# One ring of six slots for spread gates and gated activations, with a new table of front steps

## What is computed

```python
gate_v = _get_sel_gate(x, sel_v_w, rs)      # top 2 of 8 experts per head and token
gate_o = _get_sel_gate(x, sel_o_w, rs)
q = jnp.einsum('bsd,hpd->bhsp', x, q_w.reshape(H, P, D))
k = jnp.einsum('bsd,hpd->bhsp', x, k_w.reshape(H, P, D))
xv = jnp.einsum('bsd,hedp->bshep', x, v_w.reshape(H, E, D, P))
v = jnp.einsum('bshep,bshe->bhsp', xv, gate_v)
att = jax.nn.softmax(jnp.einsum('bhqp,bhkp->bhqk', q, k) * SCALE, axis=-1)
ctx = jnp.einsum('bhqk,bhkp->bqhp', att, v)
weighted = ctx[:, :, :, None, :] * gate_o[..., None]
out = jnp.einsum('bshep,hepd->bsd', weighted, o_w.reshape(H, E, P, D))
```

## Time and profile before

| | us |
|---|---|
| runs shown: median (lowest to highest) | 785.13 (782.28 to 785.24) |
| profiled execution, its own time | 786.33 |
| its span, first to last instruction | 785.0 |

### The profile page before, as it was taken

The page is one execution under the profiler, slowest core; times in us unless marked ns, Lnnn a source line. Parts: engine busy times, 40 slices in busy tenths (PEclk is TensorE's granted clock), DMA queues, the critical chain, the costliest instruction groups (busy, mean ns, idle before and its releaser), DMA issues.

```text
span 785.0 us, 14588 instructions
## 1 busy us (share of the span) xinstructions
PE 688.7 (88%) x5496; PEld 604.3 (77%) x5496; DVE 496.0 (63%) x1289; ACT 373.4 (48%) x1281; POOL 181.6 (23%) x256
## 2 busy tenths in 40 slices
PE   5768987889999998889999989699899997879887
PEld 4568886557899998587899978597899994557766
DVE  1756455847847758765676767694857857254535
ACT  2510102773351665635345576546465634646483
POOL 1000004433011131415300150335201506420040
PEclk9869999899999999889999999889999998798969
DMA  9669895007946730087475410274425700000000
GB/s 359 256 174 324 307 316 185 1 8 234 305 165 223 264 119 1 26 250 261 161 228 182 161 56 2 63 269 167 166 95 176 267 4 7 1 1 1 1 1 8
DMA packets 33190, 113.72 MB, mean 145 GB/s; under 512 B 3680, under 2 KB 7264, under 8 KB 32736
## 3 DMA queue, kind: packets, MB, share of 16 engines
q1 hardware_dynamic: 33120, 112.78, 42.3%
HBM read 111.72 MB, written 1.05 MB: 144 GB/s over the span
## 4 chain that ended last, share of the span: by engine, by line
PE 43%; DVE 25%; DMA 15%; ACT 6%; POOL 5%; issue 4%; SPq 0%; POOLq 0%; DVEq 0%
PE bank L460 24%; DMA spread<-gates_of 15%; PE f_bank L460 14%; DVE gated L1432 7%; ACT wide_b L1104 3%; PE bank L656 2%; DVE wide_b L1435 2%; POOL rstd L1323 2%; DVE x L1435 2%; PE f_bank L553 1%; DVE f_route L1432 1%; DVE max_neg L1693 1%; POOL wide_b L1332 1%; DVE f_max_neg L1511 1%; ACT f_b L1040 1%
## 5 line engine op out<-in xcount | busy, mean ns | idle before, releaser
L460 PE MATMUL f_bank<-weights,gated 128*128 128x128 f32 x2048 | 253.9, 282 | 22.8 <-DVE gated L1432 22.5
L460 PEld LDWEIGHTS f_bank<-weights,gated 128*128 128x128 f32 x2048 | 242.3, 196 | 32.2 <-issue 21.7
L1104 ACT ACTIVATE wide_b<-wide_b,max_neg 128x120 f32<-128x120 f32 x272 | 103.5, 384 | 48.1 <-DVE max_neg L1693 42.7
L1432 DVE TENSOR_TENSOR gated<-spread,f_b 128x1024 f32<-128x1024 f32 x64 | 79.5, 1258 | 44.1 <-DMA spread<-gates_of 20.4
L1432 DVE TENSOR_TENSOR gated<-spread,f_xnT 128x1024 f32<-128x1024 f32 x64 | 80.9, 1269 | 37.1 <-DMA spread<-gates_of 34.6
L1332 POOL TENSOR_TENSOR wide_b<-wide_b,row_inv 128x480 f32<-128x480 f32 x64 | 71.6, 1122 | 127.3 <-DVE row_inv L1698 127.3
L1323 POOL TENSOR_TENSOR rstd<-var_eps,w_const 128x1 f32<-128x1 f32 (+1 forms) x56 | 38.2, 683 | 251.3 <-DVE var_eps L1428 251.2
L989 ACT ACTIVATE wide_a<-bank 120x512 f32<-120x512 f32 (+4 forms) x109 | 57.6, 544 | 62.2 <-PE bank L460 23.6
L656 PE MATMUL bank<-w_const,wide_b 128*120 128x128 f32 x256 | 46.5, 319 | 11.8 <-POOL wide_b L1332 11.7
L1104 ACT ACTIVATION_READ_ACCUMULATOR wide_b<-wide_b,max_neg 128x1 f32 x272 | 51.6, 190 | 0.0
L656 PEld LDWEIGHTS bank<-w_const,wide_b 128*120 128x120 f32 x256 | 33.4, 159 | 22.9 <-issue 21.2
(11 more groups left out here) (236 smaller groups left out, 1179.0 us busy)
## 6 DMA issues: line engine op xcount, KB each, us to landing
spread<-gates_of SPq DMA_DIRECT2D x128, 512.0 KB, 5.5
weights<-in_experts SPq DMA_DIRECT2D x64, 512.0 KB, 6.4
w_L2f<-in_L2f SPq DMA_DIRECT2D x1, 2124.0 KB, 15.2
w_L3x<-in_L3x SPq DMA_DIRECT2D x1, 2108.0 KB, 19.2
wide_b<-in_raw0f SPq DMA_DIRECT2D x1, 1024.0 KB, 6.2
w_L3f<-in_L3f SPq DMA_DIRECT2D x1, 1000.0 KB, 20.5
w_L1f<-in_L1f SPq DMA_DIRECT2D x1, 516.0 KB, 9.8
x_next<-in_x SPq DMA_DIRECT2D x4, 128.0 KB, 5.0
```

The source lines that it names most:

```text
L460: return nc.tensor.matmul(o, lhsT, rhs, start=first, stop=last)
L1104: last = nc.scalar.activation(p, p, ACT.Exp, bias=max_neg[lane][:, h:h + 1], accum_out=row_sum[lane][:, h:h + 1])
L1432: return nc.vector.tensor_tensor(o, a, c, op)
```

## The change

- `spread` is gone; `gated` has six slots in place of three. The DMA of spread n writes into `gated[n % 6]` and waits until product n-6 has read the slot. DVE multiplies in place, and no longer waits for PE.
- SBUF use is the same: six tiles of 128x1024. The waits of `load_weights` stay.
- All five rows of `AHEAD` are new.

```diff
-W_SLOTS, G_SLOTS = 4, 3
+W_SLOTS, G_SLOTS = 4, 6
...
-    "PE": "24 14 8 7 11 5 3 0 3 0 0 3 0 1 3 2 0 0 3 2 0 1 0 0 0 0 0 4 0 0 1 0 2 1 4 1 2 1 0 0 1 0 0 0 0 1 0 1 1 "
...
+    "PE": "10 6 5 15 28 0 8 0 0 5 0 2 0 1 2 2 1 0 2 0 1 2 0 0 0 0 0 7 0 0 1 0 2 1 2 1 3 1 0 0 0 1 1 0 0 0 1 0 0 "
...
-    "Activation": "29 2 4 0 1 7 0 1 2 1 0 1 2 1 0 1 2 0 0 3 0 2 2 0 1 0 0 0 0 0 0 0 0 1 1 0 1 0 0 0 0 1 2 0 0 1 1 0 0 0 "
...
+    "Activation": "19 0 12 0 4 8 0 4 1 0 1 2 0 0 0 0 3 0 0 3 0 0 1 2 2 0 0 0 0 0 1 0 0 1 0 0 3 1 0 1 0 0 0 0 1 0 0 0 0 "
...
-    "DVE": "23 1 7 14 11 10 2 1 1 0 0 0 0 1 1 0 0 0 7 0 1 2 2 0 1 0 1 2 0 0 0 1 0 1 2 0 0 0 3 0 2 0 2 0 1 0 0 1 "
...
+    "DVE": "4 6 15 5 25 8 5 2 0 1 0 1 0 0 1 0 2 0 1 1 5 1 1 0 0 3 2 2 0 0 0 2 0 1 1 0 0 0 3 0 0 0 2 0 0 0 1 4 1 "
...
-    "SP": "67 25 6 18 16 18 0 1 ",
+    "SP": "67 26 15 2 23 15 3 ",
...
-        spread = [sb(f"spread{i}", [128, E * S]) for i in range(G_SLOTS)]
         gated = [sb(f"gated{i}", [128, E * S]) for i in range(G_SLOTS)]
...
                     if n >= G_SLOTS:
-                        sp.wait_ge(f_gated_ready, n - G_SLOTS + 1)
-                    sp.dma_start(spread[n % G_SLOTS][:, :],
+                        sp.wait_ge(f_expert_psum, n - G_SLOTS + 1)
+                    sp.dma_start(gated[n % G_SLOTS][:, :],
...
                         dve.wait_ge(f_spread_loaded[slot], 16 * (n // G_SLOTS + 1))
-                        if n >= G_SLOTS:
-                            dve.wait_ge(f_expert_psum, n - G_SLOTS + 1)
                         tt(gated[slot][:, :].rearrange("p (e s) -> p e s", s=S),
-                           spread[slot][:, :].rearrange("p (e s) -> p e s", s=S),
+                           gated[slot][:, :].rearrange("p (e s) -> p e s", s=S),
                            rows.unsqueeze(1).broadcast_to([128, E, S]), ALU.mult).then_inc(f_gated_ready, 1)
```

## The result

| | us |
|---|---|
| before, median of four runs (lowest to highest) | 785.09 (782.28 to 785.24) |
| after, median of four runs (lowest to highest) | 758.49 (756.85 to 760.07) |
| ratio after to before | 0.967 (0.964 to 0.970) |
| profiled execution of after: its own time, its span | 758.24, 756.9 |

The change takes 26.6 us off the median, 28.1 us off the profiled span. One of the four executions of e11_changed_again took 1308.25 us against 757.50 to 758.25 for the others, in a second and slower state of the chip, and is left out of its time.

What follows compares the result with a forecast made beforehand. It took front 0 as bound by a load-and-gating beat, B by PE, A by chains of short steps. Front 0 -5, ring -4, multiplication 0, table +3 made -6 us against the profiled 786.33; predicted 779.5, range 766 to 797.

Steps and rivals of the forecast that it cites:

- Front 0, the DMA's rate: Front 0's products: 23.3 MB at 330 GB/s, ending after 75.4 instead of 83.6 us; 8 us saved, 2 at 305 GB/s.
- Front 0, the setup: Setup work on DVE moved ahead of the first spread lengthens the chain to it: 3 us, ends 0 and 6.
- Ring, fronts 1 to 3: DVE no longer queues for PE's products; half of PE's 8.2 us of waits for gated tiles goes: -4, ends 0 and -8.
- Multiplication in place: The 128 gatings on DVE, 1.26 us each, take no longer in place: 0 us.
- The other bound, 16 us: Gatings in place at 1.35 ns per column would add 16 us to DVE, a few us of it on the chain.
- Table, A: A sections of backs 0 to 2 under the new table: 180.9 us against 182.4, by a straight line in front records.
- the line: Least-squares fit over four sections A: 40.7 us plus 0.0966 us per front record.
- the 794 case: Aligned fronts starve PE: attention steps beside the backs' chains make A 195.9 us, +13.5; 794 us in all, chance 0.24.
- the 765 case: Products fill the gaps: each A costs what back 2's does, 162.8 us together, -19.6; about 765 us in all, chance 0.10.
- Table, B: B sections of backs 0 to 2: 346.4 us against 342.0, by 87.4 us plus 0.0623 us per front record.
- Back 3: The last back, running alone with no front steps in either table: no change, near 132 us.
- the marks that the prediction set: Signs expected in the changed profile: spread start, front 0's end and DMA share, DVE waits, gating times, A, B and back 3.

Runs made afterwards that it cites:

- e11_changed_again: The changed kernel unaltered, run once more beside two other experiments; 757.6 us (median of three), ratio to before 0.965.
- e3_three_in_flight: The changed kernel, all six slots kept, but SP waits so that at most three spreads are in flight or unread; 786.2 us, ratio to before 0.997.
- e9_setup_late: The changed kernel with the first AHEAD entries of PE, Activation and DVE from before, so the late setup runs in its old place; 758.7 us, ratio 0.966.
- e1_ring_only: The changed kernel with the AHEAD table of before, so only the new ring is new; 765.2 us, ratio to before 0.971.
- e5_dve_waits_old_table: The new ring with the table of before, and DVE again waits for product n-3 before gating tile n; 767.0 us, ratio to before 0.974.
- e2_table_only: The changed kernel with the old rings (spread and gated, three slots each), so only the AHEAD table is new; 827.4 us, ratio to before 1.049.
- e4: The changed kernel, six slots kept, but DVE again waits for product n-3 before gating tile n; 804.3 us, ratio to before 1.020.

## Why the prediction was wrong, step by step

**Front 0, the DMA's rate: the step that failed first.** The sum took 330 GB/s as the most the DMA gives, since it was 98% busy at that rate, so 23.3 MB could not take less than 70.6 us. But the share is the time that packets are under way; with three loads in flight it was 0.92 to 0.98 at 330 to 333 GB/s, with five and six it is 1.02 to 1.03 at 400 to 411. The share was near its top well before the rate was. The number of loads in flight sets the rate, which e3_three_in_flight shows by changing nothing else. The trace of before had counter-evidence in a stretch that the prediction did not use, the chain ahead of the products, where other and larger loads (up to 2.1 MB, all issued by 13 us) were under way; columns as above:

```profile
20.00:25.00 5.00, 4.74 (x12) 2.61 (x13) 2.59 (x11) 0.72 (x3) 1.13 (x2) 0.64 0.99 424
25.00:30.00 5.00, 4.86 (x41) 4.67 (x42) 3.77 (x9) 2.68 (x6) 0.00 (x0) 1.00 0.99 425
```

At 425 GB/s the stretch's 23.3 MB are 55 us, below PE's 32 x 1.79 = 57 us of gated products alone, and the prediction would have named PE as the next bound. The measured time from the first product (51.16) to the end of the last (some 116.8) is 65.6 us: 57.3 for gated products at 0.112, some 5 for the 42 other records between them, and some 3 for the start, where the first 53 records take 8.88 us, 0.168 each, at a granted clock of 0.68 from 51.16 to 60 us. PE had stood idle from 45 to 51 us, waiting for the first tile.

Two pages of the Trainium skill bear on it. The prediction drew on DMA: Bandwidth & Descriptors, Specifications, with about 358 GB/s for one core. In the Trainium skill the same page's section Bandwidth has 425 GB/s for a transfer of 16 MB with the other core of the pair idle, and the Trainium skill's HBM Reference, Specifications (TRN2), says that the lower figure is each core's share when both stream. The 424 and 425 above and the 400 to 411 of front 0, in a program on one core, agree with that and exceed 358; the figure that I chose belonged to another case. The sum did not rest on it but on the 330.

**Front 0, the setup: right in its mechanism, too dear in size.** The chain was held up by what was worked out: the choice of experts starts at 28.14 us against 25.96 in the earlier trace rows, 2.2 us against 2.3. But the first spread came only 0.7 us later (45.11 against 44.40, and not at 47). That pair understates it: over all profiled executions the first spread starts at 43.1 to 45.3 us in the four kernels with the setup's old place and at 45.1 to 46.5 in the nine with the new one, 1.3 us apart on average. In between, the setup's products on PE now run just ahead of the gates' transposes, and the granted clock of 40 to 45 us is 1.00 where it was 0.50 in before; the first eight transposes of probabilities, which stand between the two of the gates, take 1.07 us against 1.94, which gives back part of the 2.2.

```profile
40.00:45.00 5.00, 2.88 (x21) 1.93 (x19) 0.65 (x3) 3.64 (x13) 0.00 (x0) 1.00 0.04 13
```

```profile
40.00:45.00 5.00, 3.51 (x17) 2.98 (x15) 3.30 (x9) 2.56 (x5) 0.00 (x0) 0.50 0.06 18
```

The first row is of after, the second of before. In e9_setup_late, with the setup in its old place, the clock of that stretch is 0.50 again, and yet its first spread starts earliest of all, at 43.11: the clock gives back less than the setup takes. That front 0 ends only 0.3 us earlier there shows besides that the start of the spreads no longer decides. Front 0 together: -5 forecast, -11.2 measured.

**Ring, fronts 1 to 3: the size came out, by luck in part.** Forecast -4, measured -4.2 in B of e1_ring_only (341.9 to 337.7), from one execution each, and the slowest of its four for e1_ring_only. PE's waits for a gated tile fell from 8.2 us to 5.2 there, less than the half that I took. And e5_dve_waits_old_table, where DVE stands 21.2 us for products again, still keeps 2.0 of the 4.2. That the gain with the old table comes from DVE's freedom is not shown.

**Multiplication in place: right.** The groups of the two gatings in the changed kernel (times are shortest, median and longest in ns, then from where to where):

```profile
L1431 DVE TENSOR_TENSOR gated<-gated,f_xnT x64: 1212/1219/1490, 49.8 to 539.7; 128x1024 f32<-128x1024 f32 x64
L1431 DVE TENSOR_TENSOR gated<-gated,f_b x64: 1193/1224/2009, 85.2 to 617.1; 128x1024 f32<-128x1024 f32 x64
```

1219 and 1224 ns are what two separate buffers took (1225 and 1225 in the trace of before). The other bound, 16 us, came from a shape of 512 columns (690 ns in place, more than half of the 1219 for 1024), and scaled its whole time by the number of columns.

**Table, A: right, and both rivals that lived on it fell.** Forecast 180.9, measured 182.0 (and 180.9 in e11_changed_again). By section the line gave 61.6, 58.5 and 60.8; measured 63.5, 58.5 and 60.0. The attention steps side by side with the back's chains neither starved PE (the 794 case) nor filled its gaps (the 765 case).

**Table, B: the step that failed second and more.** Forecast 346.4, or 342.4 with the ring's 4 us off; measured 327.6. A straight line through four points priced a record at 0.062 us on top of 87.4. That line took all time above its intercept for the price of work, and so had stalls of PE in it. In the three B sections of before PE stands idle for 5.8, 7.7 and 3.7 us by the earlier trace rows, 17.2 together; in the changed kernel for 3.0, 1.5 and 1.9, 6.4 together, with almost the same number of records (2979 against 2958). So some 10.8 of the 14.3 us are stalls that went, and the rest is busy time, 0.108 us a record against 0.110. The pace of the changed kernel's B, 327.6 us for 2979 records, 0.110 each, would bring before's records to 325.4 in place of 341.9; but this pace is that of the result itself, so that the changed kernel reaches it proves nothing. With what was known before, 0.112 us for each of the 1352 records of the front and the 1625 of the backs' own (2958 less 1333), an estimate would have been 333 us, nearer than the line's 346.4. In e1_ring_only PE's idle time in B is 14.6 us, so the ring takes 2.6 us of the stalls, and the rest went only with the new table on the ring. PE's waits for a gated tile from 117.7 to 627 us are now

```profile
PE f_bank L459 <- DVE gated L1431: 1.8, 3, 0.8
```

against 8.2 us in the earlier trace rows.

**The sum of parts.** The prediction priced ring and table each by itself and added. e1, e2, e4 and e5 show that they are one design: -17, +42, and -28 together. A sum of separate prices could not have given this; asking which waits of DVE the new order would meet in the old rings, and which in the new, would at least have shown that the table's price hangs on the ring. The ring's own part and the table's part on top of it are known only within some 7 us, as said at e2_table_only.

**Back 3.** Forecast unchanged at 132, measured 129.6. All other kernels have 128.8 to 130.2, e2_table_only with the old rings and e1_ring_only with the old table among them; only before's profiled execution has 131.7. Back 3 has the same work in all of them, and its longer section goes with the granted clock: 90.6 us at 0.85 in before, 89.2 to 89.6 at 0.86 to 0.88 in eight kernels, and 88.0 to 88.2 at 0.89 in the four others. The last line of before's and this one of e1_ring_only have the same 558 records:

```profile
679.60:767.60 88.00, 72.22 (x558) 58.91 (x558) 45.49 (x170) 47.69 (x159) 13.88 (x19) 0.89 0.01 3
```

Before has 4.0 us more of PE's busy time there and 1.4 us less idle time, so its records are slower and its stalls are not longer. In the shorter section before's 41.1 us at 0.79 stand beside 40.3 at 0.83 in after. So this part of the gain, 2.1 of the 28.1 us, goes with the clock and not with the order of the work; why the clock differs between the executions stays open.

Of the marks that the prediction set, these came as said: no DVE idle put down to PE ahead of a gating, a DMA share of 0.97 from 55 to 115 us (at least 0.95 was said), gatings of 1.22 us (1.23 to 1.27 was said), A near 61, 58 and 60. These did not: first spread at 47 (45.1), last product of front 0 at 123 (116.8), B near 115 each (109.2, 110.4, 108.0).

The rest of the miss by size, against the forecast of -6 for the profiled execution: front 0 -6.2, B -14.7 (-14.3 where the ring's -4 and the table's +4.4 had been forecast), A +1.0 (-0.5 against -1.5), back 3 -2.1, together -22.

## What to carry to other kernels

Take the DMA's ceiling from the stretch with the most loads in flight, never from a busy share beside a ring that limits them; then name the engine that is next. Before a fit prices the work that is moved into a stretch, read the bound engine's idle time at each of its points: that part is stall, which the change may remove or double. An order written by hand and the depth of its buffers are priced together, and the quickest test is the new order on the old buffers and the reverse.

## What the runs showed of the hardware that I had not expected

The rate of 512 KB loads that write one source row set to 128 partitions, with weights of 512 KB among them, rises with the number that may be in flight. The best 10 us between 60 and 110 us have 333 GB/s with three, 348 with four slots, 400 with five, 410 to 415 with six (in the seven kernels that have six slots and no other limit), and 413 with seven. The profile's DMA share does not tell these apart: it was 0.98 in before at 330, 0.99 with four slots at 348 and 1.02 at 404, so it is no measure of what is left.

With five slots the rate over 70 to 80 us is nearly as high as with six (400 against 404), and front 0 still ends 6.8 us later: a ring has to cover the stalls of a stretch, not only its best rate.

A single wait in the queue of an in-order engine cost 47 us or 2 us, with the same instructions in two orders. Some 15 of the 47 are not idle time: PE stood idle for 38.4 us in B in place of 6.4, and the rest came as slower records, at a granted clock of 0.92 to 0.99 in place of 1.00.
